# Context and sums of the attention in one matmul pass with 32x32 block transpositions, the last layer divided anew, transition and expert products merged

## What is computed

```python
x = L0(ctx, ctx, x, mask)   # 16-head cross attention, layernorm, feed-forward 256-1024-256, layernorm
x = L1(ctx, x)              # cross attention, layernorm
x = L2(x, ctx)              # causal self attention, cross attention, mixture of 8 experts, top 2
x = L3(x, ctx, ctx)         # windowed attention with one key/value head, gate, rms norm

# each attention
a = softmax(scores, axis=-1)
o = einsum('bhqk,bkhd->bqhd', a, V).reshape(B, S, D) @ Wo
# experts
combine = zeros((T, E)).at[arange(T)[:, None], topi].add(topw)
h = gelu(einsum('td,edf->etf', xf, w1) + b1[:, None, :])
eo = einsum('etf,efd->etd', h, w2) + b2[:, None, :]
# L3
gate = silu(concatenate([attn, query], -1) @ Wg + bg)
out = attn * gate + query * (1.0 - gate)
x_hat = out * rsqrt(mean(out * out, -1, keepdims=True) + EPS) * rms_w
return x_hat - mean(x_hat, axis=1, keepdims=True)
```

## Time and profile before

| | us |
|---|---|
| median of 3 runs | 2302.21 |
| the profiled execution, its time | 2305.83 |
| the profiled execution, its span | 2304.0 |
| PE busy | 2108.5 (92%) |
| DVE busy | 1644.6 (71%) |
| ACT busy | 1092.9 (47%) |
| POOL busy | 1038.3 (45%) |

### The profile page before, as it was taken

One profiled execution on the slowest core, in us unless ns is written; L12 is line 12 of the kernel. 1 busy time (PEld: TensorE's weight loads), 2 busy tenths in 40 slices (PEclk: granted clock), 3 DMA queues, 4 the chain that ended last, 5 costly groups with the idle time before them and its releaser, 6 DMA issues.

```text
span 2304.0 us, 84589 instructions
## 1 busy us (share of the span) xinstructions
PE 2108.5 (92%) x31768; PEld 1837.1 (80%) x31769; DVE 1644.6 (71%) x3373; ACT 1092.9 (47%) x2804; POOL 1038.3 (45%) x1304
## 2 busy tenths in 40 slices
PE   5999999999999999999999975999999997888897
PEld 4877877878878878878878755999999996676776
DVE  4688787787787887887887875444544446889986
ACT  2345344354454344453444433556555553555554
POOL 3445455455455454554554634110211007767763
PEclk9999999999999999999999987999999997999989
DMA  8401001001001001001000103121221112211110
GB/s 196 163 3 38 8 21 43 7 19 42 9 19 39 11 19 36 16 19 31 18 22 4 39 29 133 50 64 39 60 70 39 39 32 82 59 55 56 56 50 21
DMA packets 93477, 101.02 MB, mean 44 GB/s; under 512 B 23968, under 2 KB 84384, under 8 KB 93088
## 3 DMA queue, kind: packets, MB, share of 16 engines
q1 hardware_dynamic: 84128, 72.02, 10.4%
q0 software_dynamic: 8704, 25.19, 3.5%
q10 hardware_dynamic: 384, 0.01, 0.0%
HBM read 64.94 MB, written 32.24 MB: 42 GB/s over the span
## 4 chain that ended last, share of the span: by engine, by line
PE 56%; issue 17%; DVE 15%; ACT 5%; POOL 4%; DVEq 1%; SPq 1%; DMA 1%; POOLq 0%; ACTq 0%
PE ps_scores L1071 10%; PE ps_w L1084 9%; PE ps_o L897 8%; PE ps_scores L858 4%; ACT pt_all L1242 4%; PE ps_qk L779 4%; PE ps_qk L745 4%; DVE rs L1492 3%; PE ps_xv L685 2%; PE ps_xv L763 2%; DVE lower L1473 2%; PE ps_scores L805 1%; PE ps_scores L865 1%; PE ps_w L944 1%; POOL rstd L1940 1%
## 5 line engine op out<-in xcount | busy, mean ns | idle before, releaser
L1485 DVE TENSOR_REDUCE mb<-ps_scores 128x16 bf16<-128x2048 f32 x160 | 365.8, 2286 | 57.8 <-PE ps_scores L838 54.2
L1492 DVE RECIPROCAL rs<-ps_o 128x256 f32<-128x256 f32 x160 | 280.4, 1752 | 33.1 <-PE ps_o L897 29.0
L1242 ACT ACTIVATE pt_all<-ps_scores 128x512 f32<-128x512 f32 x512 | 263.5, 602 | 48.4 <-PE ps_scores L865 48.4
L1071 PE MATMUL ps_scores<-tiles,w_now 128*128 128x128 f32 x2272 | 267.4, 276 | 1.2 <-DVE tiles L1767 1.2
L1071 PEld LDWEIGHTS ps_scores<-tiles,w_now 128*128 128x128 f32 x2272 | 262.0, 193 | 1.8 <-issue 1.8
L1328 ACT ACTIVATE tiles<-ps_scores,b1s 128x128 f32<-128x128 f32 x568 | 154.2, 383 | 204.6 <-PE ps_scores L1071 178.8
L1940 POOL TENSOR_TENSOR rstd<-ve,neghalf 128x1 f32<-128x1 f32 x192 | 109.6, 571 | 308.0 <-DVE ve L1503 268.1
L1084 PE MATMUL ps_w<-w_split,g_split 128*128 x1704 | 224.3, 288 | 7.5 <-DVE g_split L1787 5.8
L1924 POOL TENSOR_TENSOR lower<-lower,consts 128x512 fp32r<-128x512 f32 x160 | 171.3, 1071 | 123.7 <-DVE lower L1473 77.5
L1084 PEld LDWEIGHTS ps_w<-w_split,g_split 128*128 128x128 f32 x1704 | 210.0, 192 | 12.4 <-issue 9.5
L1917 POOL TENSOR_TENSOR qbd_all<-qT,consts 128x512 fp32r<-128x512 f32 x160 | 167.3, 1046 | 104.9 <-ACT kT L1228 74.4
(11 more groups left out here) (247 smaller groups left out, 4830.2 us busy)
## 6 DMA issues: line engine op xcount, KB each, us to landing
tiles<-sorted_x SPq DMA_DIRECT2D x72, 128.0 KB, 2.0
sorted_y<-tiles SPq DMA_DIRECT2D x71, 128.0 KB, 1.7
w_experts<-in_L_xattn_e_w SPq DMA_DIRECT2D x8, 1024.0 KB, 10.4
w_raw<-in_L_xattn_e_w POOLq DMA_DIRECT2D x8, 1024.0 KB
ct_scratch<-cT SPq DMA_DIRECT2D x32, 128.0 KB, 1.7
x_scratch<-x2b_all SPq DMA_DIRECT2D x32, 128.0 KB, 1.7
arena<-x_scratch SPq DMA_DIRECT2D x32, 128.0 KB
cT<-ct_scratch SPq DMA_DIRECT2D x32, 128.0 KB, 2.1
```

The source lines that it names most:

```text
L1071: last = mm(ps_s[:, 2 * par + j // 4, P * (j % 4):P * (j % 4 + 1)], w1_now[:, par, c, P * j:P * (j + 1)], xgT[par][:, c, :], start=c == 0, ...
L1242: nc.scalar.activation(pt[:, 4 * g:4 * g + 4, :].rearrange("p h q -> p (h q)"), ps_s[:, g, :], ACT.Exp, bias=bias, scale=LAYER[l]["scale"] ...
L1485: V.tensor_reduce(mb[:].rearrange("p (g r) -> p g r", g=BANKS)[:, :, 0:SLOTS], ps_s[:].rearrange("p g (h k) -> p g h k", h=SLOTS), AX_X, A ...
L1492: V.reciprocal(rs[:], ps_o[:, 2:4, :]).then_inc(recip_ready, 1)
```

## The change

The attention's product becomes one pass. `vz` now holds each head's 16 values beside 16 ones, so that a head fills a strip of its own: 16 rows of context, 16 rows of its sum. `normalise` brings queries onto the partitions by a transposition of 32x32 blocks, takes 16 reciprocals of each partition, multiplies, and transposes back. `av` now waits for the first transposition only. `vz_evac` becomes one instruction. The router's rank matmuls take bf16 operands.

In the experts the high and low halves of `w2` lie beside each other, so that one matmul of 512 columns takes the place of two of 256; `tile_y` adds the two halves in two steps; `tile_split` has two instructions of 1024 elements for four of 512; POOL's subtractions are in halves.

In the transition the table is computed over tiles and experts at once; the tails are filled with zeros (640 rows for each expert) inside the last iteration; the constants of the last layer are folded ahead of the experts; the positions are shifted (`pos_all`) after the first tile's transpositions.

In the last layer `combine_apply` and `rms_apply` move from DVE to ACT, `finish` from ACT to DVE (with the weight of the rms norm), POOL gets one more product (`c_nb`), and the steps of `combine` and of the gate alternate on DVE. The first sequence's keys and values are projected ahead, and its scores come ahead of the second's projections.

PE's and SP's part:

```diff
             if first:
                 late_loads(tau)
+            if last and tau == TPI // 2:
+
+                sp.wait_ge(consts_ready, 1)
+                sp.wait_ge(tails_ready, 1)
+                for e in range(E):
+                    r = sp.value_load(tails[0:1, e:e + 1], min_val=0, max_val=DUMMY - TAIL)
+                    sp.dma_start(sorted_x[bass.ds(r, TAIL), :].rearrange("(a p) d -> p a d", p=P),
+                                 zeros[:].unsqueeze(1).to_broadcast([P, TAIL // P, D])).then_inc(tail_zeroed, 16)
...
-            wait(pe, ot_ready, t)
-            for kind in range(2):
-                for c in range(KC):
-                    for par in range(2):
-                        for q in range(4):
-                            h = c * HPC + 2 * q + par
-                            w = vz[p][:, h // 2, par].rearrange("p a d -> p (a d)") if kind == 0 else onz[:, par].rearrange("p a d -> p (a d)")
-                            last = mm(ps_o[32 * q:32 * q + 32, 2 * kind + c, :], w, pt[:, SLOTS * q + PAIR * c + par, :],
-                                      start=par == 0, stop=par == 1, tile_position=(0, 32 * q))
+            wait(pe, o_rows_ready, t)
+            for c in range(KC):
+                for par in range(2):
+                    for q in range(4):
+                        h = 0 if l == 4 else c * HPC + 2 * q + par
+                        last = mm(ps_o[32 * q:32 * q + 32, 2 * par + c, :], vz[p][:, h].rearrange("p a d -> p (a d)"),
+                                  pt[:, SLOTS * q + PAIR * c + par, :], start=True, stop=True, tile_position=(0, 32 * q))
...
+            def part(g_, j):
+                n = 2 * D if g_ == 0 else D
+                return mm(ps_w[:, 0:n], g_split[:, g_, j, :].bitcast(F32R),
+                          w2_split[:, bass.ds(odd * (2 * FC * D) + j * 2 * D, n)].bitcast(F32R),
+                          start=j == 0 and g_ == 0, stop=j == FC - 1 and g_ == 0)
             for j in range(FC):
-                for g_, w_ in ((0, 0), (0, 1), (1, 0)):
-                    last = mm(ps_w[:, 0:D], g_split[:, g_, j, :].bitcast(F32R),
-                              w2_split[:, bass.ds(odd * (2 * FC * D) + (w_ * FC + j) * D, D)].bitcast(F32R),
-                              start=j == 0 and g_ + w_ == 0, stop=j == FC - 1 and g_ == 1)
+                for g_ in (0, 1) if j < FC - 1 else (1, 0):
+                    last = part(g_, j)
```

DVE, attention:

```diff
+            src = ps_xv[:, D:2 * D].rearrange("p (h d) -> p h d", d=HD)
             bv = LAYER[l]["bv"]
-            for par in range(2):
-                if bv is None:
-                    last = V.tensor_copy(vz[p][:, :, par, par, :], src[:, :, par, :])
-                else:
-                    last = V.tensor_tensor(vz[p][:, :, par, par, :], src[:, :, par, :],
-                                           rows[bv].rearrange("p (h two d) -> p h two d", two=2, d=HD)[:, :, par, :], ALU.add)
+            if bv is None:
+                last = V.tensor_copy(vz[p][:, :, 0, :], src)
+            else:
+                last = V.tensor_tensor(vz[p][:, :, 0, :], src, rows[bv].rearrange("p (h d) -> p h d", d=HD), ALU.add)
...
-            V.reciprocal(rs[:], ps_o[:, 2:4, :]).then_inc(recip_ready, 1)
+
+            V.transpose(o_rows.rearrange("p a b r -> p (a b r)"), ps_o[:].rearrange("p a q -> p (a q)")).then_inc(o_rows_ready, 1)
+            dve.wait_ge(o_rows_ready, t + 1)
+            V.reciprocal(o_inv[:], o_rows[:, :, :, HD]).then_inc(recip_ready, 1)
             dve.wait_ge(recip_ready, t + 1)
-            V.tensor_tensor(oT[:], ps_o[:, 0:2, :], rs[:], ALU.mult).then_inc(ot_ready, 1)
+            V.tensor_tensor(o_rows[:, 0].rearrange("p b (par d) -> p par b d", par=PAIR), o_rows[:, :, :, 0:HD],
+                            o_inv[:].unsqueeze(3).to_broadcast([P, PAIR, KC * BANKS, HD]), ALU.mult).then_inc(o_scaled, 1)
+            dve.wait_ge(o_scaled, t + 1)
+            V.transpose(oT[:].rearrange("p c q -> p (c q)"), o_rows[:, 0].rearrange("p b r -> p (b r)")).then_inc(ot_ready, 1)
```

DVE, table of tiles:

```diff
+        V.tensor_scalar(shift[:], n_t, float(P), -float(SPAN), ALU.mult, ALU.add)
+        tlink(V.tensor_tensor_scan(incl, ones, n_t, 0.0, ALU.mult, ALU.add))
+
+
+        tlink(V.tensor_tensor(past[:], tile_iota.unsqueeze(2).to_broadcast([P, TILES, E]), by_tile(incl), ALU.is_ge))
+        tlink(V.tensor_tensor(steps[:], past[:], by_tile(shift[:]), ALU.mult))
+        V.tensor_reduce(eid, past[:], AX_X, ALU.add)
+        tlink(V.tensor_reduce(row_, steps[:], AX_X, ALU.add))
+        tlink(V.scalar_tensor_tensor(tbi[:, 0, 0:TILES], tile_iota, float(P), row_, ALU.mult, ALU.subtract))
+        V.tensor_scalar_min(tbi[:, 1, 0:TILES], eid, float(E - 1))
+        V.tensor_copy(tbi[:, 2, TILES - 3:TILES], tbi[:, 0, TILES - 1:TILES].to_broadcast([P, 3]))
```

DVE, experts:

```diff
+            wait(dve, b_down, k + 1)
+            wait(dve, b_stored[par], 16 * use)
+            V.tensor_tensor(ys[par], ps_w[:, 0:D], b2.rearrange("p e d -> p (e d)")[:, bass.ds(e * D, D)], ALU.add).then_inc(b_part, 1)
+            wait_apart(dve, b_part, k + 1)
+            V.tensor_tensor(ys[par], ps_w[:, D:2 * D], ys[par], ALU.add).then_inc(b_y, 1)
+
+        def tile_split(k):
+            wait(dve, b_gelu, k + 1)
+            wait(dve, b_down, k)
+            V.tensor_copy(g_split[:, 0].bitcast(F32R), gT).then_inc(b_high, 1)
+            wait_apart(dve, b_high, k + 1)
+            V.tensor_tensor(g_split[:, 1].bitcast(F32R), gT, g_split[:, 0], ALU.subtract).then_inc(b_split, 1)
```

Last layer, ACT and DVE, then the order on DVE and POOL:

```diff
-            nc.scalar.copy(fin[n["p"]], ps_w[:, D:2 * D]).then_inc(c_fin, 1)
+            wait(act, c_rstd, b + 1)
+            wait(act, c_xr, b - NS + 1)
+            nc.scalar.activation(xn[n["s"]][:], yb[n["p"]][:], ACT.Identity, bias=c_nb[:], scale=rstd[2][:]).then_inc(c_xn, 1)
+
+        def rms_apply(n):
+            b = n["b"]
+            wait(act, c_rms, b + 1)
+            wait(act, c_mean, b - 1)
+            nc.scalar.activation(xh[n["p"]], go, ACT.Identity, bias=0.0, scale=rstd[3][:]).then_inc(c_xh, 1)
...
+            wait_apart(dve, c_ln, COMBINE * b + 3)
             V.bn_aggr(mv[2][:], st6[2][:]).then_inc(c_ln, 1)
-            dve.wait_ge(c_ln, 6 * b + 4)
+            wait(dve, c_rstd, b)
+            dve.wait_ge(c_ln, COMBINE * b + 4)
+            V.tensor_scalar_mul(c_nm[:], mv[2][:, 0:1], -1.0)
             V.tensor_scalar_add(ve[2][:], mv[2][:, 1:2], LN_EPS).then_inc(c_ln, 1)
...
+
+        def finish(n, last_at):
...
+            wait(dve, c_mean, b + 1)
+            wait(dve, c_at, last_at)
+            wait(dve, c_out[n["p"]], 16 * n["h"])
+            V.tensor_tensor(fin[n["p"]], ps_w[:, D:2 * D], row3["L3_xattn_rms_w"][:], ALU.mult).then_inc(c_fin, 1)
```

```diff
+                    part(c(2))
+            if f_["ok"]:
+                finish(f_, g_["b"] + 1 if g_["ok"] else B)
...
-                combine_apply(nn)
             if prev["ok"]:
                 normalise(prev)
             if g_["ok"]:
                 gate_open(g_)
-            if m_["ok"]:
-                rms_apply(m_)
+
             if c(3)["ok"]:
-                combine(c(3))
+                combine_first(c(3))
             if g_["ok"]:
-                gate_apply(g_)
+                gate_silu(g_)
+            if c(3)["ok"]:
+                combine_second(c(3))
+            if g_["ok"]:
+                gate_product(g_)
+            if c(3)["ok"]:
+                combine_stats(c(3))
+            if g_["ok"]:
+                gate_sum(g_)
+            if c(3)["ok"]:
+                combine_moments(c(3))
...
+            wait(pool, c_xn, b)
+            root(2, c_ln, COMBINE * b + 5, c_root_done)
+            wait(pool, c_root_done, b + 1)
+            G.tensor_tensor(c_nb[:], c_nm[:], rstd[2][:], ALU.mult).then_inc(c_rstd, 1)
...
+                wait(pool, c_xh, h_["b"])
+                G.tensor_tensor(rstd[3][:], ve[3][:], neghalf[:], ALU.pow).then_inc(c_rms, 1)
+            if nxt["ok"]:
+                c_residual(nxt)
+            if g_["ok"]:
+                difference(g_)
+
             if c(4)["ok"]:
                 gather(c(4))
```

300 lines of the change are left out of this document (142 added, 158 removed).

## The result

The changed kernel takes 2241.38 us, median of 4 runs (2237.64 to 2245.86), against 2302.62 for the kernel before; the ratio is 0.9727, 95% interval 0.9713 to 0.9741. The forecast was 2215 with a range of 2175 to 2262. The profiled execution has a span of 2239.3 us, 64.7 less than before. Measured again later, together with edited kernels, the same program took 2218.26 us (2215.01 to 2227.50; ratio 0.9645, 0.9616 to 0.9674), and its profile has a span of 2218.6.

A forecast was written before the change was run, and what follows sets the result against it. Bounds: a loop alternating DVE and PE in attention, PE in the experts, DVE leading in the last layer. Terms −25 −17 −7 −5 −33 = −87 took 2305.83 to 2218.8 profiled, 2215 on the median; range 2175 to 2262.

The forecast's parts named there:

- PE's pass fills time that ends with `xn`: Attention's four feed-forward slots an iteration: removing the 1.07 us ones pass gains 0, since `xn` is late next.
- Rival 3: Attention: all PE time comes back, 128 tasks giving 137 us instead of 25, whole 2103; chance 0.05.
- Slots 1 and 2, and `vz`: Attention: 1.4 us an iteration from PE reaching maxima earlier in two slots, 0.7 from merged `vz`, 1.0 from ten others.
- The new `normalise`, 2.0 us: Every task: transpositions 0.69 and 0.42, reciprocal 0.25, product 0.42, plus waits; 0.2 us less, counted in the last layer alone.
- rival 4: Every slot's loop: block transpositions cost several times the maxima's rate, making the kernel slower, 2481 us; chance 0.03.
- Rival 1: Feed-forward and last-layer slots: POOL locks out DVE's new product in SBUF, costing 34 us, whole 2249; chance 0.20.
- Transition, −7: Between attention and experts: a faster table saves 13 us, about half counted because scatter and position shift precede `down`.
- Experts, −17: Experts: eight merged 512-column matmuls and eight of 256 make `down` 0.24 us shorter in each of 71 tiles.
- To the last layer, −5: From experts to last layer: constants folded ahead of the experts and first sequence projected ahead; ends −2 and −8.
- Last layer, −33: Last layer: DVE work falls from 10.50 to 9.7 us, slot to 10.75, gaining 1.03 in 32 slots; ends −5 and −60.
- DVE leads: Last layer: DVE is the busiest engine, 168.01 of 188.48 us for 16 slots, 10.50 of 11.78 a slot.
- Rival 2: Last layer: one sequence's chain through four engines keeps the pace, slot 11.6, gain 5 for 33, whole 2243; chance 0.20.

The follow-up runs named there:

- gate_first: Changed kernel with the second half of the gate's product put ahead of the maxima's transposition on PE in the last layer; 2204.62 us.
- av_twice: Changed kernel with the pass of context and sums issued twice, giving PE back the time of the removed ones pass; 2228.71 us.

## Why the prediction was right or wrong

The forecast of 2215 lies 26 us below the first measurement and 3 below the second; both are in the range. In part this is luck: two terms, the experts' and the last layer's, came near their size by other ways than the forecast's. And the 0.2% that I took for the reach of a measurement was too little, since the same program differed by 1.0% between two. Step by step:

- **PE's pass fills time that ends with `xn`; nothing gained in feed-forward slots.** Right: 495.5 and 496.6 us in those slots for 496.1, and PE idle where the pass was. An engine busy in 95% of a stage gave up a tenth of its work for 1.5% of the time. What the text did not see is the clock: in `gate_first`, with none of these slots at the lower clock, they take 491.5. Rival 3 asked for 137 us and got at most 26. Its 137, like the 1.07 us a task, was itself a duration; by the spacing (573.19 to 574.08 us before) a pass costs 0.9.
- **Slots 1 and 2, and `vz`.** Forecast 3.1 us an iteration; the first profile has 2.46 in the iteration shown, the second −0.5 to 4.3 from one iteration to another. Slots 1 and 2 gave 7.9 us in all for 11 forecast.
- **The new `normalise`, 2.0 us.** The transpositions' price, taken from the maxima's rate, is right to 0.03 us; rival 4 falls, with a slope now known: doubling one transposition costs 30 to 53 us. The two durations (710 ns for 512 elements, 446 for 256) give 1.03 ns an element and 0.18 us fixed, if one rate holds for both. The Trainium skill ("VectorE: DVE Perf Modes", The three transpose paths) gives 311 ns for 128x128 in two-byte elements. My estimate from the two durations is 0.31 us for 128 elements of four bytes, which agrees, though no run has that size; the sentence of the prediction that added the figure six times over counted the fixed part six times.
- **Rival 1, the product locked out by POOL.** The mechanism is there, the mean 816 ns for 426 at the least, and falls to 423 with an operand in PSUM. Its price of 34 us was wrong: I placed it in the feed-forward slots behind `xn`, but it falls mostly in ordinary slots (882 ns in the mean, for 674 in feed-forward slots), where DVE's wait covers it. What does cost is the hold-up of the cast beside POOL in the experts, 6.0 to 7.7 us for each tile that it meets. The Trainium skill ("SBUF — State Buffer", SBUF: two separate sides) states that VectorE with two SBUF inputs and GpSimd take a shared port pair as an exclusive lock. The product's durations with two operands in SBUF and with one agree; nothing here shows the port itself.
- **Transition, −7.** Measured −8.2 and −7.9, as 11 us to the first `up` and 3 to 4 given back before the first `down`, by the shift of the positions, as the text had it.
- **Experts, −17.** Too large, and from the wrong place. The step that failed is the term 0.24 us x 71: it took 3.12 / 24 = 131 ns for a matmul, but the duration includes the last one's way through the array. The text ahead of the prediction makes the same slip, where it calls the duration over the count the spacing. By the spacing (a `down` starts at 1601.75 us before, the next `up` at 1604.73) 24 cost 2.98, 124 ns each; the changed kernel's 16 have 2.87. The merged product gives 8.4 us; 5.7 come from six slow tiles that I had not looked for. `tile_split`, whose saving I counted at nothing, is what was slow in them, and in the held-up tiles DVE does end the experts' wait.
- **To the last layer, −5.** 2.9 and 3.4: within the ends.
- **Last layer, −33.** 27.9 and 42.7, and the step behind it failed: "DVE leads", 10.50 us becomes 9.7 with half of the idle time gone. DVE fell to 8.5, more than counted, the slot to 10.04, not 10.75, and the slot no longer follows DVE: with 0.7 more or 0.3 more on DVE, or 0.9 more on PE, it stays or even falls. The starting value was off too: 11.78 us holds for the 16 slots read, at a granted clock of 0.95, and the mean of the whole layer was 11.37.

What brought 11.4 down to 10.04 can be read from the loop in three parts. From a maxima's start to their transposition on PE there are 3.21 us before and 3.20 after, and from there to the start of the next scores 6.14 in both, in the steady slots at the full clock (six slots before, partly at the lower clock, have 5.8 to 10.6). The third part, from the scores' start to the next maxima, is the one that changed: 1.4 to 3.5 us in most slots before, 0.70 after. Before, DVE was still at the combination and the gate (L1864 is the gate's last step) when the scores were ready:

```profile
2056.58 0.39 PE L838 MATMUL ps_scores<-kT,qbd_all 32*128 32x128 bf16 x16
...
2057.82 0.43 DVE L1864 TENSOR_TENSOR arena<-arena,xr 128x256 f32<-128x256 f32 x1
...
2058.81 2.29 DVE L1485 TENSOR_REDUCE mb<-ps_scores 128x16 bf16<-128x2048 f32 x1 [0.56 <-DVE arena L1864]
```

So DVE did lead, as the prediction says, but only as long as its queue ended behind the scores; once it ended ahead of them, PE's 6.14 us set the pace, and DVE work can be given back for nothing. Rival 2's ground, an order and not an amount, describes the loop that is left, though its 11.6 is wrong. Which of the remaining edits shortened DVE's queue enough stays open: the product and either move can be taken back alone, and nothing else was.

## What to carry to other kernels

Ask of each busy engine what its next wait ends with: work that stands in a wait's shadow can be removed or doubled without moving the time, even at 95% busy, and the cheap test is to issue it twice. In a loop that alternates between engines, order the queues so that work that nobody waits for stands where the engine waits; that gained 14 us with no instruction saved, while `finish`, put ahead of the loop's first step on DVE, lost 0.24 us a slot. Split a loop's slot into the parts between its hand-overs, before and after: the part that changed names the engine that held it up. Take a matmul's price from the spacing of two runs, not from a run's duration over its count.

## What the runs showed of the hardware

- Block transpositions in fp32 on VectorE took 710 ns for 512 elements and 446 for 256, which is 1.03 ns an element and 0.18 us fixed, and were steady (704 to 720 ns over 160).
- A product with both operands in SBUF took 426 to 1311 ns beside POOL's work; with one operand in PSUM 423 in the mean.
- A cast of 1024 elements from SBUF to SBUF on VectorE, 0.68 us by itself, took 5.46 to 5.75 beside a row of POOL's subtractions of 0.45 us each, in seven places of four profiles: it lay beside 13 or 14 of them and ended behind them.
- With PE idle for 146 to 154 us of the attention, TensorE's granted clock was at the lower level in one to nine stretches (seven profiles of the same attention code); with PE idle for 66 and 67 us (the kernel before, `av_twice`) in none.
- Sixteen fp32r matmuls, half of them with 512 columns and half with 256, have the spacing 2.87 us, 24 with 256 columns 2.97 (1606.08 to 1609.05): a merged pair saves some 12 ns.
- One profile has waits of ACT of up to 2.4 us without a releaser in every fourth slot of the last layer, some 15 us of 2240; the 13 others have none, one of them of the same program. What it is stays open.
